# Router and sort spread between the convolution's products, and the experts' unit steps set in triples

## What is computed

```python
# 1 convolution of 1x1 kernels on the group-normed input
info = relu(info_w @ x + info_b); mask = sigmoid(mask_w @ x + mask_b)      # 16 and 16 channels
x = x + relu(out_w @ (mask[:, :, None] * info[:, None]) + out_b)            # 256 products per token
# 2 linear attention on layer-normed tokens, 8 heads
Q, K = elu(q) + 1, elu(k) + 1
msg = layernorm((Q @ (K.T @ v)) / (Q @ K.sum()) @ Wm) * g1 + b1
t = t + x_ln + layernorm(relu(concat(x_ln, msg) @ W1) @ W2) * g2 + b2
# 3 mixture of 8 experts, the two best of a token by a softmax router
top2_vals, top2_idx = top_k(softmax(xf @ gate_w + gate_b), 2)
t = t + sum(weight[e] * (gelu(xf @ W1[e] + b1[e]) @ W2[e] + b2[e]) for e in the two)
```

## Time and profile before

| | us |
|---|---|
| median of 3 runs | 1300.73 (1295.26 to 1302.85) |
| the profiled execution | 1301.52 |
| its span in the profile | 1299.7 |
| PE busy | 1002.7 |
| DVE busy | 756.4 |
| ACT busy | 545.4 |
| POOL busy | 480.2 |

### The profile page before, as it was taken

The page is one execution under the profiler, slowest core; times in us unless marked ns, Lnnn a source line. Parts: engine busy times, 40 slices in busy tenths (PEclk is TensorE's granted clock), DMA queues, the critical chain, the costliest instruction groups (busy, mean ns, idle before and its releaser), DMA issues.

```text
span 1299.7 us, 34961 instructions
## 1 busy us (share of the span) xinstructions
PE 1002.7 (77%) x14091; PEld 628.9 (48%) x14091; DVE 756.4 (58%) x1737; ACT 545.4 (42%) x836; POOL 480.2 (37%) x482
## 2 busy tenths in 40 slices
PE   5888582877998699868897699869986899742796
PEld 2453251454655366544755466546654565531322
DVE  5554762277646765477637766586647664630255
ACT  2245230652555245542565254543555255510343
POOL 0010037002755075703763075605571385300450
PEclk7788866895999789987999699987999699965798
DMA  4530000663576446654557356653656255689311
GB/s 142 154 93 1 1 7 28 172 178 97 133 188 157 132 127 180 161 139 113 148 151 185 101 154 173 157 158 104 182 148 179 71 160 149 172 202 233 82 36 49
DMA packets 258933, 168.88 MB, mean 130 GB/s; under 512 B 156500, under 2 KB 244052, under 8 KB 258772
## 3 DMA queue, kind: packets, MB, share of 16 engines
q1 hardware_dynamic: 244436, 151.70, 43.4%
q0 software_dynamic: 14336, 14.94, 4.8%
HBM read 133.12 MB, written 33.42 MB: 128 GB/s over the span
## 4 chain that ended last, share of the span: by engine, by line
PE 44%; DVE 23%; issue 6%; SPq 5%; ACT 4%; DMA 1%; POOL 1%; DVEq 0%; ACTq 0%
PE HP L1073 4%; PE R L788 3%; PE HP L1053 3%; PE R L813 3%; PE HP L1091 3%; PE R L777 2%; DVE CWB L1752 2%; PE R L953 2%; PE R L962 2%; PE R L955 2%; PE R L842 2%; PE R L866 2%; PE R L875 2%; PE HP L1029 2%; PE HP L1040 2%
## 5 line engine op out<-in xcount | busy, mean ns | idle before, releaser
L1334 POOL DMA_INDIRECT slots_hbm<-CWB,IDX x224 | 219.8, 981 | 397.3 <-DVE IDX L1738 331.1
L1345 POOL DMA_INDIRECT CWB<-y_hbm,IDX x224 | 219.8, 981 | 223.5 <-issue 116.0
L1263 ACT ACTIVATE H<-HP 128x1024 f32<-128x1024 f32 x84 | 83.1, 989 | 204.6 <-PE HP L1053 203.2
L1752 DVE TENSOR_TENSOR CWB<-HP,CWB 128x512 f32<-128x512 f32 x84 | 55.9, 665 | 162.3 <-PE HP L1073 161.8
L1040 PE MATMUL HP<-W,CWB 128*128 128x128 f32 x322 | 59.4, 311 | 107.4 <-DMA CWB<-slots_hbm 67.3
L1053 PE MATMUL HP<-CWB 64*64 64x64 f32 x5152 | 103.7, 234 | 9.6 <-DVE OF_BLOCK L1733 5.1
L1053 PEld LDWEIGHTS HP<-CWB 64*64 64x64 f32 x5152 | 91.8, 146 | 35.9 <-issue 31.0
L1040 PEld LDWEIGHTS HP<-W,CWB 128*128 128x128 f32 x322 | 37.7, 154 | 141.2 <-issue 72.1
L1255 ACT ACTIVATE CWB<-HP 128x512 f32<-128x512 f32 x84 | 49.2, 586 | 126.9 <-PE HP L1040 126.7
L1073 PE MATMUL HP<-CWB,H 128*64 128x64 f32 x2576 | 101.5, 239 | 0.0
L1073 PEld LDWEIGHTS HP<-CWB,H 128*64 128x64 f32 x2576 | 94.4, 155 | 0.0
(11 more groups left out here) (262 smaller groups left out, 1980.6 us busy)
## 6 DMA issues: line engine op xcount, KB each, us to landing
CWB<-pairs_hbm SPq DMA_DIRECT2D x644, 128.0 KB
CWB<-slots_hbm SPq DMA_DIRECT2D x77, 132.0 KB, 2.8
CWB<-slots_hbm SPq DMA_DIRECT2D x77, 128.0 KB, 2.4
y_hbm<-CWB SPq DMA_DIRECT2D x77, 128.0 KB
X<-x SPq DMA_DIRECT2D x14, 512.0 KB, 4.4
out<-XB SPq DMA_DIRECT2D x11, 512.0 KB, 4.1
BIG<-gates_hbm SPq DMA_DIRECT2D x16, 256.0 KB, 8.3
slots_hbm<-CWB,IDX POOLq DMA_INDIRECT x224
```

The lines of the kernel that those rows point to most:

```text
L1263: f(H[:, n % 2, :, some], L1.rearrange("p (r t) -> p r t", r=2)[:, :, some], ACT.Gelu).then_inc(gelu_done, 1)
L1334: nc.gpsimd.indirect_dma_start(out=slots_hbm[a % 2], in_=XFT[:, t, :], in_offset=None, out_offset=bass.IndirectOffsetOnAxis(ap=IDX[:, a % ...
L1345: nc.gpsimd.indirect_dma_start(out=YG[:, t, :], out_offset=None, in_=y_hbm[a % 2], in_offset=bass.IndirectOffsetOnAxis(ap=IDX[:, a % 2, t: ...
L1752: v.tensor_tensor(YT[:, there, :, :], YPS[:, there, :, :], SLT[:, n % 3, there, P:P + 2].unsqueeze(3).broadcast_to([P, columns(u), 2, C]), ...
```

## The change

- SCHEDULE is rewritten. The unit steps stand as B, T, A behind one stage (B of unit n, T of unit n+2, A of unit n+1), at eleven places of a turn, some incomplete. The router's and the sort's stages are spread: choose_1 behind info_mask_1, choose_2 behind low_0.0, classes behind high_0.0, sort_1 behind info_1.0, choose_3 and gate_rows behind low_1.0, shares behind high_1.0, sort_3 behind conv_out.1.
- choose_2 is cut in two; its second part, from the wait for the exponentials on, is choose_3.
- gate_rows is left to the dense group. What waited for its copy in other turns waits for lg_shifted (the router's logits read out of PSUM).
- In turn 1 the unit steps of group 0 that would stand behind first_unit are left out; they are issued ahead of everything in turn 2 (LATE).

```diff
@@ -74,23 +74,24 @@
 SCHEDULE = [
-    ("channel_stats", "KA"), ("gates", "K"), ("gate_tokens", "TB"), ("gate_exp", ""), ("group_stats", "K"),
-    ("group_norm", "AK"), ("choose_1", ""), ("info_mask_0", "TB"), ("choose_2", "A"), ("classes", ""),
-    ("info_mask_1", "FT"), ("gate_rows", "B"), ("shares", ""), ("sort_1", ""), ("info_0.1", ""), ("info_0.0", "F"),
-    ("sort_2", ""), ("low_0.1", ""), ("low_0.0", "F"), ("sort_3", ""), ("high_0.1", ""), ("high_0.0", "AF"),
-    ("info_1.1", ""), ("info_1.0", "T"), ("low_1.1", ""), ("low_1.0", "B"), ("high_1.1", ""), ("high_1.0", "A"),
-    ("conv_out.1", "T"), ("conv_out.0", ""), ("centre_1.1", ""), ("store", ""), ("centre_1.0", "B"),
-    ("rstd_1", "A"), ("norm_1.0", "T"), ("norm_1.1", "B"), ("features_1.0", ""), ("features_1.1", "A"),
-    ("query.1", ""), ("query.0", "T"), ("key.1", "B"), ("key.0", ""), ("key_value.1", ""), ("key_value.0", "A"),
-    ("kv_turn.1", ""), ("kv_turn.0", ""), ("kv_values.1", ""), ("kv_values.0", "B"), ("denominator", ""),
-    ("numerator.0", ""), ("numerator.1", ""), ("first_unit", ""), ("attended.0", ""), ("attended.1", "T"),
-    ("message.1", ""), ("message.0", "A"),
-    ("variance_2", "T"), ("rstd_2", "B"), ("spread_2", ""), ("norm_2.0", "A"),
+    ("channel_stats", "KBTA"), ("gates", "K"), ("gate_tokens", ""), ("group_stats", "BTAK"), ("gate_exp", ""),
+    ("group_norm", "BTAK"), ("info_mask_0", ""), ("info_mask_1", "BTA"), ("choose_1", ""),
+    ("info_0.1", ""), ("info_0.0", "F"),
+    ("low_0.1", ""), ("low_0.0", "F"), ("choose_2", ""), ("high_0.1", ""), ("high_0.0", "BTA"), ("classes", ""),
+    ("info_1.1", ""), ("info_1.0", ""), ("sort_1", ""), ("low_1.1", "F"), ("low_1.0", ""), ("choose_3", ""), ("gate_rows", ""),
+    ("sort_2", ""), ("high_1.1", "F"), ("high_1.0", ""), ("shares", ""), ("conv_out.1", ""), ("sort_3", ""),
+    ("conv_out.0", ""), ("centre_1.1", ""), ("store", ""), ("centre_1.0", "BTA"),
+    ("rstd_1", ""), ("norm_1.0", ""), ("norm_1.1", "BTA"), ("features_1.0", ""), ("features_1.1", ""),
+    ("query.1", ""), ("query.0", "BA"), ("key.1", ""), ("key.0", ""), ("key_value.1", ""), ("key_value.0", ""),
+    ("kv_turn.1", ""), ("kv_turn.0", "B"), ("kv_values.1", ""), ("kv_values.0", ""), ("denominator", ""),
+    ("numerator.0", ""), ("numerator.1", ""), ("first_unit", ""), ("attended.0", ""), ("attended.1", "TTA"),
+    ("message.1", ""), ("message.0", ""),
+    ("variance_2", "BTA"), ("rstd_2", ""), ("spread_2", ""), ("norm_2.0", ""),
     ("hidden_0.0", ""), ("norm_2.1", ""), ("hidden_0.1", ""), ("hidden_1.0", ""),
-    ("hidden_1.1", "T"), ("hidden_out.1", ""), ("hidden_out.0", "B"),
-    ("variance_3", "A"), ("rstd_3", "T"), ("spread_3", ""), ("norm_3.0", "B"),
-    ("centre_4.0", ""), ("norm_3.1", ""), ("centre_4.1", "A"),
-    ("variance_4", "T"), ("rstd_4", "B"), ("spread_4", ""), ("norm_4.0", ""),
+    ("hidden_1.1", ""), ("hidden_out.1", ""), ("hidden_out.0", ""),
+    ("variance_3", "BTA"), ("rstd_3", ""), ("spread_3", ""), ("norm_3.0", ""),
+    ("centre_4.0", ""), ("norm_3.1", ""), ("centre_4.1", ""),
+    ("variance_4", "BTA"), ("rstd_4", ""), ("spread_4", ""), ("norm_4.0", ""),
     ("norm_4.1", ""),
 ]
...
@@ -497,6 +499,12 @@
             done = dict(BEGUN, K=0, F=0)
+            if b == 1:
+                done = {step: 0 for step in done}
+                for step in LATE:
+                    if steps.get(step):
+                        steps[step](done[step])
+                    done[step] += 1
             for name, letters in SCHEDULE:
...
                 for step in letters:
-                    if steps.get(step):
+                    if steps.get(step) and not (a == 1 and step in "TAB"):
                         steps[step](done[step])
...
@@ -766,7 +774,7 @@
                             if exists(a - 1) and a != EARLY:
-                                pe.wait_ge(cwt_done, a)
+                                pe.wait_ge(lg_shifted, nth(a, G - 1))
...
@@ -1660,6 +1669,8 @@
                     router_link(v.tensor_tensor(gt(2), gt(2), gt(4), ALU.add))
+
+                def choose_3():
                     dve.wait_ge(gate_exp, a + 1)
...
-                    "choose_1": choose_1, "choose_2": choose_2, "gate_rows": gate_rows,
+                    "choose_1": choose_1, "choose_2": choose_2, "choose_3": choose_3,
+                    **({"gate_rows": gate_rows} if a == DENSE else {}),
```

16 lines of the change are left out of this document (9 added, 7 removed), and 2 rows, old and new, of the table OPENING.

## The result

The changed kernel takes **1490.7 us** (1485.9 to 1493.1) where the kernel before takes 1298.8 (1295.3 to 1302.9) on the same chip: a ratio of **1.147**, 95% interval 1.142 to 1.152. The forecast was 1447 with a range of 1375 to 1485. So the sign and most of the size came as worked out, but 44 us are missing from the sum, and the time lies 6 us above the range.

The account below looks back on a forecast made before the run. No engine is full (PE 77%, DVE 58%), so waits inside a turn set the time. 1299.7 + 161 (six turns) - 12 (turn 1) - 1 (turn 8) - 1 (opening) = 1446.7 us; forecast 1447, range 1375 to 1485.

Parts of the forecast that it names:

- rival A: Combination before the root mostly hidden, or DVE reaches IDX earlier: 1340 to 1405 us; chance 0.18.
- Rival C: Not slower: the router's gap pays and rows arrive in time, if IDX comes by 44; chance 0.05 up to 1300.
- The six turns: Turns 2 to 7: 169.6 us each, + 28.1; + 161 in all after allowances for turns 2 and 7.
- the clock's term: Low clock behind the wait for rows: 2.0 us a turn over T, message and A; bounds 0 and 7.
- that of the second half: Message to next turn's start: 51.5 us instead of 44.4, each root beginning 2.6 later; bounds 44.4 and 53.
- The roots' own part, + 7.1: Three roots in a turn's second half, each delayed by the combination ahead of it on DVE: + 7.1 us a turn.
- The base of 44.4: Message to next turn's start in the kernel before, 44.4 us, to which the roots' delay was added.
- Turn 1 and the opening: First turn with its unit steps behind attention: - 12 us; opening with choose_3 instead of gate_rows: - 1.
- 44.4 - 3 later, at 244: Turn 1: time from 203.2, without PE's wait, to where the batch of four triples begins.
- Behind turn 7: Turn 8: broadcast of the gates later in SP's queue, dense units' start moving little; - 1 us, bounds - 8 and + 8.
- The 59.7: First half of a turn: IDX at 59.7 us from the turn's start, where it was 44.5; bounds 44 and 63.
- rival D: Worse, over 1485: IDX at 63 with the earlier low clock behind the wait, 1495 us; chance 0.06.

Follow-up runs that it names:

- e1_root_first: The changed kernel with B, T, A moved from behind variance_2, 3 and 4 to behind rstd_2, 3 and 4: 1430.8 us, ratio 1.106.
- e2_sort_early: The changed kernel with router and sort back at about their earlier places, triples kept: 1407.3 us, ratio 1.088.
- e7_spread_alone: Router and sort as in the change, but single unit letters at about the places of the kernel before, no LATE: 1354.5 us, ratio 1.045.
- e9_pieces: The kernel of e8_candidate with GpSimd's residual add cut into four instructions of 256 columns per image: 1264.6 us, 0.974 to the kernel before.
- e10_before_late: The kernel before with only the LATE batch of turn 1 added: 1292.3 us, ratio 0.9956.
- e5_rows_first: The changed kernel with SP requesting rows of the next group's units 1 and 2 ahead of their weight blocks: 1470.3 us, ratio 1.135.
- e8_candidate: The kernel before with the router spread, sort_3 behind low_1.1, single letters, gate_rows for the dense group only, rows before weights, X later: 1295.0 us, ratio 0.9993.

## Why the prediction was right or wrong

**Right: where the time goes.** The forecast put the loss on two mechanisms, rows late behind a late sort and the combination ahead of the root, and rejected rival A (half of it) because the queues leave no way round. The marks that it named are there: waits of 8.65 and 9.08 us for rows (6.5 and 8.5 said), 103 us of them in six turns (90 said), IDX at 60.7 (59.7), unit 1's transposes 55.7 behind it (54.6), 2.2 us of idle time at each spread (2.5). Turn 2 near 263 is the mark that is not. Undoing the one gives back 54 us (e1_root_first), undoing the other 77 (e2_sort_early), and doing the spread by itself costs 58 (e7_spread_alone). Rival C, that the spread pays, falls for this schedule, but its condition, the index in time, was the right one: e9_pieces meets it and gains.

**Wrong: the sizes of three terms.** In the span 1446.7 was worked out and 1488.2 came: 41.5 us. Another 2.2 lie in what is around the span and in the rounding of the forecast.

- **The six turns: 26.** A turn was 169.6 and is 174.1. IDX came 1.0 late and unit 1's rows 1.1, of which 0.8 is their load: it took 4.1 us from the request to the transposes (731.89 to 735.98), and the sum had 3.25. From unit 1's transposes to the next turn the sum has 1.8 + 2.0 + 51.5 = 55.3, and it took 57.8: 2.5 more. Six times 4.6 is 28; turn 2 saved 1.8 and not 4, turn 7 6.5 and not 3.5. The step that failed for the 2.5 is the clock's term with that of the second half. For message the clock costs 1.2, as in the sum; for T and A together 1.1, where the sum had 0.8. The roots' own part, + 7.1, is right (6.9 by e1_root_first), though its working does not give it: three times 2.6 less 0.3 is 6.9 or 7.5. But the three idle stretches of 2.2 us are not only idle time: with them the stretch is granted 0.84 to 0.86, without them 0.97, and the matmuls behind them take up to twice their time, which is the 4.1 us that no term had. The base of 44.4 hid part of it: that stretch has 689 matmuls, the new one 586. e1_root_first has 43.8 with message 1.1 slow, so 42.6, and 42.6 + 1.2 + 6.9 + 4.1 = 54.8 is what was measured. The forecast asked for the clock behind each long wait, and not what short waits do to a stretch that had been at full clock. (For the long waits it had 27.59 us as the one case of the kernel before; that kernel has a second, 36.12 us at 1192.91.)
- **Turn 1 and the opening: 14.** The forecast had - 12 and - 1, and + 0.7 came. The step that failed is "44.4 - 3 later, at 244": the batch begins at 249.9, since message and what follows it, with nothing between, take 46.7 us from 203.2 and not 41.4. The batch takes 21.8 (19 said), with one wait of 1.98 us for rows in it. So turn 2 starts at 271.7, not 263. The rest is that a triple now stands between that turn's first K and its gates: 7.8 us in place of 1.6, for which the sum had 2; and the opening gave nothing, not 1. e10_before_late shows the same chain by itself, 49 us at 0.78. A stretch that was read with the units' steps in it does not shrink by their length when they are taken out.
- **Behind turn 7: 1.6.** - 1 was said, + 0.6 came.

**IDX, right in part by luck.** The 59.7 is a sum of steps of which several missed and cancelled. The first replication came at 26.7 into the turn and not 23, behind four triples at SP's pace; DVE made up half of that, and conv_out.1 started at 49.8 (47.9 said). It took 5.4 us (L796 at 669.43, behind a wait of 2.35 for DVE) and not 3.65. PE's part of sort_3 took 2.8 (674.81 to 677.56) and not 5.0.

**The bound above.** 1485 was the forecast's own upper end, and rival D above it asked for an index at 63 together with the clock of the earlier trace rows behind the waits; it had 0.06. What came was neither, but smaller errors of one sign, + 26 and + 14. Where six turns repeat a term, the range has to be as wide as six times what the parts of one turn may miss together.

The Trainium skill ("TensorE: Matmul & The Clock Gate", A second HAM failure mode: psum-queue depth-cycling) tells of a kernel in which frequent small idle stretches between groups of matmuls make the clock go up and down, and throughput pays. The trace agrees: in the second half the granted clock is 0.84 with three idle stretches of 2.2 us. The prediction weighed only that page's section on long waits for data.

**What stays open.** The 52 us of the triples with the root first are not taken apart, nor are the 19 to 27 us by which the change costs more than its parts. Why unit 1's rows take 4.1 us from the request in the changed kernel and 5.6 in e5_rows_first, and unit 0's 2.9 and 3.8, was not tried.

## What to carry to other kernels

A step that starts a long chain on other queues (index, scatter, rows: here 55 us) has a due time, and filling a gap of 6.5 us with it is worth nothing if it is moved past that time; spread what has slack (the choice) and leave on time what has none (the sort). A small idle stretch that repeats in a stretch of dense matmuls costs its length and the clock of the matmuls around it, here 2.3 us and another 1.4, and work taken out of the gaps of another chain can take that chain's clock with it (turn 1: 0.78 from message on in e10_before_late, 0.97 before). When a shortened part gives nothing back, look behind it for an instruction that takes many times its usual time: the gain may have been spent on a new collision, as in e8_candidate, and be had for a cut into pieces.

## What the runs showed of the hardware that I had not expected

- **VectorE held beside GpSimd.** While GpSimd ran its two adds of 1,024 columns (4.66 us together), an add of VectorE with two inputs in SBUF took 4.91 us and not 0.29; with eight adds of 256 columns (0.7 us each) it took 0.86. The Trainium skill ("SBUF — State Buffer", SBUF: two separate sides) describes this: the two engines share a pair of ports under an exclusive lock for a whole instruction, against operations of VectorE in a two-port mode or with two inputs in SBUF. The trace agrees that VectorE is shut out and not merely slowed, and differs in how long: the hold goes further than one instruction. It lasted through both adds in e8_candidate, and through the rest of both for a product of the key sums in the kernel before (642.15 to 646.06, where the adds run from 641.34 to 646.0). Which of the two kinds that product is, with one tensor in SBUF and a scalar in PSUM, no run shows. A copy out of PSUM beside the same adds was not held (L1589 at 641.94, 0.29 us).
- **The clock follows short waits.** The same matmuls from message to the next turn (584 to 586 in the records) kept PE busy 35.0 us (clock 0.97) without waits of 2.2 us for roots, and 38.8 (0.86), 39.2 (0.85) and 40.0 (0.84) with them. The long waits just before account for the last step only, 39.2 to 40.0, where message went from 3.70 to 4.88 us.
- **Useless work ahead of a wait.** 28 transposes of the identity ahead of each of two waits for rows took message from 4.88 to 3.70 us in three of the five turns 2 to 6, and 8 to 9 us off the whole kernel, although they compute nothing.
